# Layer 2 attention: the values normed in place by GpSimd, VectorE and ScalarE together, five, three and four blocks of each group of twelve

## What is computed

```
cn = (context - mean) * rsqrt(var + 1e-6) * lnc_s + lnc_b
q, k, v = heads(ln(x) @ Wq), heads(cn @ Wkv)        # 16 heads of 64
k, v = null row put ahead of k and v                 # 1501 keys
attn = softmax(where(mask, 0.25 * q @ k.T, -max))
out = ln(heads_out(attn @ v) @ Wo)
```

## Time and profile before

| | us |
|---|---|
| median of 3 runs | 2520.2 (2518.51 to 2523.51) |
| profiled execution, its own time | 2526.13 |
| its span | 2524.3 |
| TensorE, VectorE, ScalarE, GpSimd busy | 2008.6, 1418.6, 1258.0, 1368.9 |
| GpSimd's norming of the values (L1707) | 617.1 in 768 instructions |

### The profile page before, as it was taken

One profiled execution on the slowest core, in us unless ns is written; L12 is line 12 of the kernel. 1 busy time (PEld: TensorE's weight loads), 2 busy tenths in 40 slices (PEclk: granted clock), 3 DMA queues, 4 the chain that ended last, 5 costly groups with the idle time before them and its releaser, 6 DMA issues. The chain is left out here.

```text
span 2524.3 us, 52181 instructions
## 1 busy us (share of the span) xinstructions
PE 2008.6 (80%) x21121; PEld 1411.6 (56%) x21121; DVE 1418.6 (56%) x2765; ACT 1258.0 (50%) x2169; POOL 1368.9 (54%) x1176
## 2 busy tenths in 40 slices
PE   6999999589979968766666665666686788999997
PEld 3777777468855546544444444444455445777774
DVE  5777776889835445433333333334350556777775
ACT  5777776357632255333333333333350146777773
POOL 7565651267729239777666666666666015443410
PEclk8999999689989879887887877878887888999998
DMA  5555442334321233222323322333310025444430
GB/s 159 149 143 150 134 132 69 88 105 141 92 54 40 82 106 93 79 77 76 88 77 88 88 87 78 89 89 89 89 50 25 17 80 145 137 138 135 141 93 9
DMA packets 105520, 240.03 MB, mean 95 GB/s; under 512 B 45689, under 2 KB 54929, under 8 KB 105025
## 3 DMA queue, kind: packets, MB, share of 16 engines
q1 hardware_dynamic: 105280, 236.69, 32.9%
HBM read 155.38 MB, written 0.65 MB: 62 GB/s over the span
## 5 line engine op out<-in xcount | busy, mean ns | idle before, releaser
L1615 PE MATMUL L2ps<-L2keys,L2qz 128*128 128x384 f32 x896 | 360.2, 549 | 330.5 <-DVE L2negmax L1806 329.8
L1707 POOL TENSOR_SCALAR L2values<-L2values,L2value_stats 128x127 f32<-128x127 f32 x768 | 617.1, 847 | 0.0
L1615 PEld LDWEIGHTS L2ps<-L2keys,L2qz 128*128 128x128 f32 x896 | 176.3, 207 | 474.9 <-DVE L2negmax L1806 336.9
L1631 PE MATMUL L2ps<-L2work,L2values 32*128 32x224 f32 x6144 | 334.5, 365 | 41.0 <-POOL L2values L1707 36.1
L1631 PEld LDWEIGHTS L2ps<-L2work,L2values 32*128 32x128 f32 x6144 | 295.4, 192 | 106.3 <-issue 58.8
L1816 DVE STREAM_TRANSPOSE L2work<-L2work 128x1568 f32<-128x1568 f32 x112 | 202.7, 1810 | 123.1 <-PE L2ps L1631 121.5
L1806 DVE CUSTOM_DVE_ANT_0 L2work<-L2ps,L2maskadd,L2big 128x1536 f32<-128x1536 f32 x112 | 203.6, 1818 | 119.1 <-PE L2ps L1615 119.1
L1744 ACT ACTIVATE L2work<-L2work,L2negmax 128x1536 f32<-128x1536 f32 x112 | 176.2, 1573 | 134.9 <-DVE L2negmax L1806 134.7
L1749 ACT ACTIVATE L2work<-L2work,L2rinv 128x1536 f32<-128x1536 f32 x112 | 176.8, 1579 | 116.9 <-DVE L2rinv L1821 116.9
L654 ACT ACTIVATE L3probsT<-L3ps 128x448 f32<-128x448 f32 x384 | 196.3, 547 | 72.5 <-PE L3ps L511 67.8
L654 ACT ACTIVATE L0probsT<-L0ps 128x448 f32<-128x448 f32 x384 | 198.3, 552 | 47.7 <-PE L0ps L511 46.7
(11 more groups left out here) (481 smaller groups left out, 4072.5 us busy)
## 6 DMA issues: line engine op xcount, KB each, us to landing
L2values<-in_ctx SPq DMA_DIRECT2D x192, 192.0 KB, 3.6
L0key_stack<-L0key_parts SPq DMA_DIRECT2D x192, 187.5 KB
L3key_stack<-L3key_parts SPq DMA_DIRECT2D x192, 187.5 KB
L0ctxT<-in_ctxT SPq DMA_DIRECT2D x16, 750.0 KB, 4.4
L1rawT<-in_ctxT SPq DMA_DIRECT2D x16, 750.0 KB, 6.6
L2mean_spread<-L_moments SPq DMA_DIRECT2D x16, 750.0 KB, 7.2
L3ctxT<-in_ctxT SPq DMA_DIRECT2D x16, 750.0 KB, 4.4
L2wqk<-L_moments SPq DMA_DIRECT2D x15, 750.0 KB, 27.1
```

Source lines behind the costliest of these rows:

```text
L1615: last = nc.tensor.matmul(PS[:, score_bank(m) + w, 0:NCH * BW], tile_rows(m), key_window(b, w), start=True, stop=True)
L1631: last = nc.tensor.matmul(PS[:, 4 + a, 0:RT * BW], V[a * BW:(a + 1) * BW, n, :], block_cells(a, b, n), start=n == 0, stop=n == BLOCKS - 1, ...
L1707: last = nc.gpsimd.tensor_scalar(x, x, VST[:, 0, w, b, c:c + 1], VST[:, 1, w, b, c:c + 1], ALU.subtract, ALU.mult)
```

## The change

Of each group of 12 blocks GpSimd norms 5, VectorE 3 and ScalarE 4. TensorE waits for all three. So that ScalarE can do it in one instruction, the norm is now x * rstd + offset; the offsets -mean * rstd are made once by VectorE, in one instruction after the twelfth of 16 parts of the queries. VectorE and ScalarE have their groups at fixed steps (`values_due`): batch 0 in steps 0 to 3, group w of batch b + 1 in step 7b + 11 + 2w, at the end of the step's work. GpSimd norms the first two groups ahead of the keys of batch 1. SyncE's transfers of the first batch stand in another order; from batch 1 on the order is the old one. The matmul of the output bias streams the same column 128 times instead of once.

```diff
+POOL_CHUNKS, DVE_CHUNKS, ACT_CHUNKS = range(5), range(5, 8), range(8, NCH)
...
+        def values_due(n):
+            if n < WINDOWS:
+                return [(0, n)]
+            b, t = divmod(n - RT - 4, RT)
+            return [(b + 1, t // 2)] if 0 <= b and b + 1 < B and t % 2 == 0 and t // 2 < WINDOWS else []
...
-            for w in range(WINDOWS):
-                load_values(0, w)
+            load_values(0, 0)
             for a in range(4):
                 at = a * BW + LAST_KEYS
                 sp.dma_start(V[at:at + 1, BLOCKS - 1, :], k.ident[P - 1:P, :]).then_inc(s.null_rows, 16)
-            for b in range(B):
+            load_values(0, 1)
+            load_keys(1)
+            load_values(0, 2)
+            load_values(0, 3)
+            load_moments(1)
+            load_mask(1)
+            for b in range(1, B):
...
-                pe.wait_ge(s.v_ready, WINDOWS * b + blocks[-1] // NCH + 1)
+                groups = WINDOWS * b + blocks[-1] // NCH + 1
+                pe.wait_ge(s.v_pool, groups)
+                pe.wait_ge(s.v_act, groups)
+                pe.wait_ge(s.v_dve, groups)
...
-                last = nc.tensor.matmul(PS[:, 4, 0:1], W[:, 3, h, :], U[:, 1, h:h + 1], start=h == 0, stop=h == H - 1)
+                last = nc.tensor.matmul(PS[:, 4, 0:P], W[:, 3, h, :], U[:, 1, h:h + 1].to_broadcast([HD, P]), start=h == 0, stop=h == H - 1)
...
-                for c in range(NCH):
+                for c in POOL_CHUNKS:
                     x = V[:, w * NCH + c, 0:P - 1]
-                    last = nc.gpsimd.tensor_scalar(x, x, VST[:, 0, w, b, c:c + 1], VST[:, 1, w, b, c:c + 1],
-                                                   ALU.subtract, ALU.mult)
-                last.then_inc(s.v_ready, 1)
+                    last = nc.gpsimd.tensor_scalar(x, x, VST[:, 1, w, b, c:c + 1], VST[:, 0, w, b, c:c + 1], ALU.mult, ALU.add)
+                last.then_inc(s.v_pool, 1)
...
-            for b in range(B):
+            normalise_values(0, 0)
+            normalise_values(0, 1)
+            normalise_keys(1)
+            normalise_values(0, 2)
+            normalise_values(0, 3)
+            for b in range(1, B):
...
+            def normalise_values(b, w):
+                act.wait_ge(values_loaded[w], 64 * (b + 1))
+                for c in ACT_CHUNKS:
+                    x = V[:, w * NCH + c, 0:P - 1]
+                    last = nc.scalar.activation(x, x, ACT.Identity, bias=VST[:, 0, w, b, c:c + 1], scale=VST[:, 1, w, b, c:c + 1])
+                last.then_inc(s.v_act, 1)
...
                 if t == 2 and b + 1 < B:
                     mask(b + 1)
+                if n == 0:
+                    act.wait_ge(s.offsets_ready, 1)
+                for v in values_due(n):
+                    normalise_values(*v)
...
+            def normalise_values(b, w):
+                dve.wait_ge(values_loaded[w], 64 * (b + 1))
+                for c in DVE_CHUNKS:
+                    x = V[:, w * NCH + c, 0:P - 1]
+                    last = nc.vector.tensor_scalar(x, x, VST[:, 1, w, b, c:c + 1], VST[:, 0, w, b, c:c + 1], ALU.mult, ALU.add)
+                last.then_inc(s.v_dve, 1)
...
+                if h == 11:
+                    dve.wait_ge(s.stats_spread, 16 * 2 * WINDOWS * 4)
+                    nc.vector.scalar_tensor_tensor(VST[:, 0], VST[:, 0], -1.0, VST[:, 1], ALU.mult, ALU.mult).then_inc(s.offsets_ready, 1)
...
-            for n in range(TILES + 1):
+            for n in range(TILES + LAG):
...
-                if n:
+                if 0 < n <= TILES:
                     turn(n - 1)
                 if n < TILES:
                     invert(n)
+                for v in values_due(n):
+                    normalise_values(*v)
```

More of the change, by code:

```diff
@@ L1485, in attention_16_wide_heads @@
                        "values_loaded0 values_loaded1 values_loaded2 values_loaded3 mask_loaded null_rows null_column constants margins mask_ready "
-                       "v_zeroed stats_zeroed stats_spread v_ready moments_filled moments_ready moments_stored slot_ready keys_loaded0 keys_loaded1 spread_loaded keys_moved keys_scaled "
+                       "v_zeroed stats_zeroed stats_spread offsets_ready v_pool v_act v_dve moments_filled moments_ready moments_stored slot_ready keys_loaded0 keys_loaded1 spread_loaded keys_moved keys_scaled "
                        "scores_filled max_done exp_done rinv_ready scaled turned pv_done heads_ready out_filled out_ready dve_chain")
@@ L1599, in _ @@
                     load_mask(b + 1)
-                if b:
-                    for w in range(WINDOWS):
-                        load_values(b, w)
+                for w in range(WINDOWS):
+                    load_values(b, w)
         @block.tensor
@@ L1727, in _ @@
             normalise_keys(0)
-            pool.wait_ge(s.stats_spread, 16 * 2 * WINDOWS * 4)
+            pool.wait_ge(s.offsets_ready, 1)
             pool.wait_ge(s.null_column, 2)
             pool.wait_ge(s.null_rows, 64)
-            for b in range(B):
+            normalise_values(0, 0)
[4 more added lines that the diff above has]
+            for b in range(1, B):
                 if b + 1 < B:
```

## The result

| | us |
|---|---|
| before, 4 runs | 2521.7 (2518.5 to 2523.5) |
| after, 4 runs | 2554.1 (2550.6 to 2559.1) |
| ratio | 1.0131 (95%: 1.0110 to 1.0152) |
| profiled execution after, its span | 2555.2, 2553.4 |

The change costs 1.3%: 2554 us where 2569 was forecast, inside the range. In the spans it is 2553.4 - 2524.3 = 29.1 us; the medians differ by 32.4, since the profiled execution before lay 4.4 us above its median and that after 1.1.

The account below looks back on a forecast made before the run. Bound: a loop of about 42 us of transfers and 25 us of chain, without GpSimd. Loop 48, first batch +2.2, last two batches -1.6 sum to +49 us: 2569 us against 2520.2, range 2523 to 2594.

Parts of the forecast that it names:

- The place and the sign: In the batch loop: GpSimd has no part; VectorE's norming between reciprocal and maximum lengthens it 13 times, so slower (0.82).
- step 17: Step 7b + 3 of any batch b; VectorE's three norming instructions there were to cost 3.7 us a batch, 48 us.
- The hold-up: In step 17, VectorE's first norming instruction waits 2.3 us on average for GpSimd's key pass and ends 0.12 later.
- the two take turns: In step 17, VectorE's second instruction waits for GpSimd's copy (0.2 + 0.12), its third for a block (0.80 + 0.12).
- GpSimd's block: GpSimd's norming of one block of values, taken at 0.80 us.
- Batch 0: First batch: VectorE's norming ahead of a maximum beside key passes costs 1.6 us, GpSimd's wait of 1.04 saved; together +2.2.
- The tail: Last two batches: batch 14's sum ends 3.4 us later, batch 15's last group saves 5.0; together -1.6.
- Not held up: Rival, 22%: VectorE's three instructions in step 17 aren't held up by GpSimd; 13 x 0.84 = 11 us, 2530 us.
- Off the chain: Rival, 7%: step 17's groups are off the chain, so shorter norming cuts TensorE's waits; faster, 2490 us.
- cancels: Rival, 9%: groups fall into unseen gaps, and the end's saving is lost in step 108; 2520 us, within 5.

Follow-up runs that it names:

- experiment 1: Changed kernel with VectorE's three blocks of the values' last group done one step later, behind the next reciprocal: 2515.3 us, ratio 0.9972.
- experiment 3: Changed kernel with VectorE's blocks given to GpSimd (GpSimd eight, ScalarE four, VectorE none): 2514.8 us, ratio 0.9970.
- experiment 2: Changed kernel with one wait added, so that GpSimd's key passes begin only after the maximum of the step behind step 17: 2539.9 us, ratio 1.0071.
- experiment 4: Kernel before with GpSimd's twelve blocks of a group done as multiply then add instead of subtract then multiply: 2513.1 us, ratio 0.9964.
- experiment 5: Kernel before with GpSimd's twelve blocks of a group done by six pairs of operations, two blocks each: one run, 2518.6 us.
- experiment 7: Kernel before with each transfer of values made as two, the first 16 rows and the rest: 2203.8 us, ratio 0.8740.

## Why the prediction was right, and where its sizes were off

**The place and the sign: right.** It said that GpSimd is not in the loop, that the mask's landing would stay where it was, and that VectorE's three instructions of step 17 lengthen the loop 13 times. The time from seventh part to mask stayed at 44.7, and experiments 1 and 3 take the loss away by touching only these instructions.

**The hold-up: right for the first instruction, wrong for the others.** The prediction had 2.3 + 0.1 = 2.4 us for the first, which was to end 0.1 behind the pass. It took 2.05 us with one key buffer and 3.09 with the other, 2.5 on average over the 13 batches, and ended 0.1 behind the pass. Experiment 2 shows that it is the key pass. The failed step is "the two take turns: VectorE's second instruction waits for the copy (0.2 + 0.12), its third for a block (0.80 + 0.12)": both take 0.33 us. There is a turn, but with the parts exchanged: GpSimd's block waits (0.64 us in place of 0.47), off the loop. The step was drawn from the earlier trace rows, in which both GpSimd instructions are tensor_tensor longer than 1 us. The sum also rounded up: 2.3 + 0.1 + 0.3 + 0.9 is 3.6 and not 3.7, and 13 times that is 47. A batch costs 2.7 us: 35.1 in place of 48 (the groups of 2.56 and 3.60 would make 3.0; 0.3 of it is taken up between mask and seventh part, which no run isolates).

**GpSimd's block: mis-sized.** "0.80" came from the blocks of the kernel before; in the new order of operations a block takes 0.47 (experiments 4 and 5). I had read the swap from subtract and multiply to multiply and add as the same work.

**Batch 0:** 1.1 us against 2.2. The three at 932.78 take 1.03 us and not 1.6, and besides the wait of 1.04 another one of TensorE is gone, 0.66 us for the keys that GpSimd norms, which the prediction had not counted.

**The tail:** -6.6 against -1.6. The last group is normed in 2.6 us against 4.8, and the sum of batch 14 ends 1.5 us later than before, counted from the last seventh part, against 3.4. The last sum itself takes 7.01 us in place of 7.71, which the prediction had not counted.

The sum of the three, 1.1 + 35.1 - 6.6 = 29.6, is within 0.5 us what the spans show (29.1), where 49 was forecast. All three terms came out below their forecast, so the errors do not cancel; the range was wide enough to hold them. *Not held up* would have given 2530, and 2554 lies 24 above it. *Off the chain* and *cancels* were wrong: the waits for GpSimd do shrink (36.1 to 12.6), but the tail gains only 6.6 us.

**What the prediction left unasked:** it read the low share of the DMA engines in the earlier trace rows as a given. The transfers behind that row were worth 12.6% (experiment 7), the change 1.3%.

## What to carry to other kernels

Before work is spread over more engines, look whether the loop waits for the engine that is relieved; and if not, where the helpers' instructions land: three instructions of 0.33 us between a reciprocal and a maximum cost 35 us, and one step later nothing. When an edit shares work and rewrites it at the same time, time the rewriting alone; here one engine with the cheaper pair of operations beat three. And when a queue moves 30 GB/s with its engines at a share of 0.09, look at the row counts of the transfers in front first.

## What the runs showed of the hardware that I had not expected

A subtraction makes a GpSimd tensor_scalar of 128 x 127 float32 take 832 to 853 ns; multiply and add, in any order, take 479 to 483. A GpSimd tensor_tensor of 127 x 1500 stops a tensor_scalar or scalar_tensor_tensor of VectorE on 128 x 127 in SBUF until it ends (3.1 us in the change), and of three in a row one got through between two such passes (experiment 2). GpSimd's blocks of 128 x 127 lengthen them little: a group beside them took 1.08 us, against 0.83 with GpSimd at rest; and VectorE's instructions lengthen a block in their turn, 0.64 us against 0.47. And splitting each transfer of values in two, so that none has 29 rows, took 12.6% off a kernel whose busy shares gave no hint of it.
